# A pause after every sixteen router gathers in a graph, attention and mixture-of-experts kernel

## What is computed

```python
h = (x_flat @ W_gat).reshape(M, HEADS, NUM_EXPERTS)
a_src = (h * att_src).sum(-1)
a_dst = (h * att_dst).sum(-1)
e = jax.nn.leaky_relu(a_src[src] + a_dst[dst], negative_slope=0.2)
e_max = jax.ops.segment_max(e, dst, num_segments=M)
ee = jnp.exp(e - e_max[dst])
denom = jax.ops.segment_sum(ee, dst, num_segments=M)
alpha = ee / (denom[dst] + 1e-16)
msg = h[src] * alpha[:, :, None]
agg = jax.ops.segment_sum(msg, dst, num_segments=M).reshape(M, HEADS * NUM_EXPERTS) + b_gat
...
topk_s, topk_i = jax.lax.top_k(scores, TOP_K)
w = jax.nn.softmax(topk_s, axis=-1)
...
for ei in range(NUM_EXPERTS):
    g = jnp.where(topk_i == ei, w, 0.0).sum(-1)
    hh = jax.nn.gelu(x @ W1[ei] + b1[ei], approximate=False)
    out = out + g[..., None] * (hh @ W2[ei] + b2[ei])
```

## Time and profile before

| | |
|---|---|
| median of 3 runs | 5559.33 us |
| lowest and highest | 5557.41 and 5565.59 us |
| the profiled execution, its own time | 5560.58 us |
| its span in the profile | 5558.8 us |
| mean granted TensorE clock | 0.801 |
| busy: PE, DVE, ACT, POOL | 63%, 37%, 14%, 51% |
| gathers of line 1353 | 1024 |

### The profile page before, as it was taken

How to read it: one execution, slowest core, us unless ns; L and a number is a source line. 1 busy time by engine, 2 the same in 40 slices (tenths; PEclk the granted TensorE clock), 3 DMA queues, 4 the chain that set the end, 5 groups by cost and what they waited for, 6 DMA issues and landing times. The chain is left out here.

```text
span 5558.8 us, 46231 instructions
## 1 busy us (share of the span) xinstructions
PE 3511.5 (63%) x12937; PEld 2291.2 (41%) x12938; DVE 2083.0 (37%) x4892; ACT 802.4 (14%) x1970; POOL 2839.8 (51%) x2937
## 2 busy tenths in 40 slices
PE   0688888888577767777242766666666666669300
PEld 0455555555455545555121443434343434346200
DVE  5455566565566555444010111112011111103278
ACT  4111111111011111111010101111111111112000
POOL 2666666666666666666657144444445353530420
PEclk6898999899788888888675888788877878789755
DMA  7444444444455555655121111111111111111297
GB/s 254 116 112 111 114 113 113 110 112 111 112 133 148 148 145 149 166 152 151 20 62 19 32 46 35 42 39 43 38 42 46 35 46 36 46 31 63 87 255 257
DMA packets 381413, 540.56 MB, mean 97 GB/s; under 512 B 120315, under 2 KB 297819, under 8 KB 381144
## 3 DMA queue, kind: packets, MB, share of 16 engines
q0 software_dynamic: 119136, 234.44, 19.2%
q1 hardware_dynamic: 243119, 288.12, 16.2%
q10 hardware_dynamic: 19016, 16.48, 0.9%
HBM read 392.03 MB, written 146.74 MB: 97 GB/s over the span
## 5 line engine op out<-in xcount | busy, mean ns | idle before, releaser
L787 POOL DMA_INDIRECT rows<-xn_rows,gsrc x1664 | 1611.5, 968 | 902.0 <-issue 458.8
L1353 POOL DMA_INDIRECT nb<-route_rows,idx x1024 | 1001.5, 978 | 1087.4 <-DVE msg L1428 772.7
L1092 PE MATMUL PS<-rows,oh 128*128 128x257 f32 x3328 | 908.3, 426 | 339.9 <-issue 215.3
L1682 PE MATMUL PS<-arena,hid 128*125 128x256 f32 x3200 | 773.2, 400 | 524.3 <-ACT hid L1643 311.5
L1674 PE MATMUL PS<-x2g,arena 128*128 128x500 f32 x1600 | 759.4, 634 | 314.8 <-issue 154.5
L1682 PEld LDWEIGHTS PS<-arena,hid 128*125 128x125 f32 x3200 | 633.5, 199 | 680.5 <-issue 577.6
L1092 PEld LDWEIGHTS PS<-rows,oh 128*128 128x128 f32 x3328 | 693.4, 214 | 470.9 <-issue 284.3
L1617 DVE TENSOR_TENSOR y_sb<-PS,b_b 125x512 f32<-125x512 f32 x200 | 128.7, 686 | 2010.5 <-PE PS L1682 1466.4
L1674 PEld LDWEIGHTS PS<-x2g,arena 128*128 128x128 f32 x1600 | 321.2, 204 | 732.1 <-issue 540.1
L1643 ACT ACTIVATE hid<-PS,b_sb 128x500 f32<-128x500 f32 x400 | 270.2, 678 | 1551.1 <-PE PS L1674 762.5
L1164 PE MATMUL PS<-own_w,p_t 128*125 128x512 f32 x400 | 228.8, 656 | 77.6 <-ACT s_t L1052 45.4
(11 more groups left out here) (304 smaller groups left out, 3088.6 us busy)
## 6 DMA issues: line engine op xcount, KB each, us to landing
y_rows<-y_sb SPq DMA_DIRECT2D x100, 512.0 KB
arena<-y_rows SPq DMA_DIRECT2D x100, 512.0 KB
rows<-xn_rows,gsrc POOLq DMA_INDIRECT x1664
nb<-route_rows,idx POOLq DMA_INDIRECT x1024
sum_rows<-kept SPq DMA_DIRECT2D x104, 128.5 KB
x_rows<-x SPq DMA_DIRECT2D x100, 128.0 KB
hid<-x_rows SPq DMA_DIRECT2D x100, 128.0 KB
m_in<-sum_rows SPq DMA_DIRECT2D x100, 125.5 KB
```

The source lines that it names most:

```text
L787: pool.indirect_dma_start(out=rows[w][h][:, q, 0:D], out_offset=None, in_=xn_rows, in_offset=bass.IndirectOffsetOnAxis(ap=gsrc[:, s * HU + ...
L1092: last = mm(SUM[:, 0:D + 1], oh[w][h][:, q, :], rows[w][h][:, q, :], start=h == 0 and q == 0, stop=h == 1 and q == HU - 1)
L1353: pool.indirect_dma_start(out=nb[b % NBUF][:, c, :], out_offset=None, in_=route_rows, in_offset=bass.IndirectOffsetOnAxis(ap=idx[:, b * W ...
L1682: last = mm(Y[j % 2][e // 2][0:NP, (e % 2) * D:(e % 2 + 1) * D], hid[:, 4 * e + k, j * NP:(j + 1) * NP], w2_sb[:, e, k, :], start=k == 0, ...
```

## The change

With `REST = 16`, every sixteenth gather of line 1353 no longer waits for the gather four before it but for all four semaphores, that is until every gather issued so far has landed. The very first gather of all is left out. The other gathers wait as before. No instruction is added, removed or moved, and the tables and buffers stay as they are.

```diff
@@ -48,6 +48,7 @@
 AHEAD = 4
+REST = 16
 EVEN = 112
@@ -1348,7 +1349,10 @@
                     if b >= NBUF:
                         pool.wait_ge(s_nbf, b - NBUF + 1)
                     for c in range(W):
-                        if b or c >= AHEAD:
+                        if (b or c) and c % REST == 0:
+                            for q in range(AHEAD):
+                                pool.wait_ge(s_nb[q], (b * W + c) // AHEAD * 16)
+                        elif b or c >= AHEAD:
                             pool.wait_ge(s_nb[c % AHEAD], (b * W + c) // AHEAD * 16)
                         pool.indirect_dma_start(out=nb[b % NBUF][:, c, :], out_offset=None, in_=route_rows,
                                                 in_offset=bass.IndirectOffsetOnAxis(ap=idx[:, b * W + c:b * W + c + 1], axis=0)
```

## The result

| | before | after |
|---|---|---|
| median | 5562.46 us (4 runs) | 5330.73 us (4 runs) |
| lowest and highest | 5557.41 and 5567.54 us | 5323.38 and 5332.99 us |
| span of the profiled execution | 5558.8 us | 5331.2 us |
| mean granted TensorE clock | 0.801 | 0.821 |

The ratio is 0.9581, with a 95% interval of 0.9567 to 0.9596. The change takes 232 us off, where the prediction had 180. The lines of the changed file stand four further down: the gather is line 1357, the first layer 1678, the second 1686, the gelu 1647, `msg` 1432.

The account below looks back on a forecast made before the run. Gathers issued faster than their shared cost were taken to squeeze PE in the expert stage. Thirteen bursts giving 130 us, the first 22, and 10 to 50 from running ahead became -180: 5560 - 180 = 5380 us, range 4690 to 5480.

Parts of the forecast that it names:

- What bounds the kernel: Expert stage: PE alone needs 1388 of 2347 us; 959 are lost while GpSimd's gathers run.
- the backlog: Gathers cost 1.40 us of something shared, issued each 1.25: each adds 0.15 us, served one us per us in pauses.
- The pause: GpSimd's wait at every sixteenth gather: adds 1.2 to 1.96 us, taken as 1.45, 50 times.
- The curve of the squeeze: PE's us per matmul by backlog: none below about 1.8, 0.87 at 2.0, 1.58 at 2.6, 2.80 from 4.7.
- the squeeze: While gathers run, and somewhat after, all that PE completes comes through at 2.80 us a matmul at worst.
- The sum: Expert stage: some 10 us for each of 13 bursts, 22 for the first, plus running ahead: -180 us; chance 0.58.
- PE running ahead: Expert stage: what PE can make up by running ahead of its completions adds 10 to 50 us of gain.
- What costs nothing: Waits beginning batches 3 to 15, 13 places: hidden under VectorE's until the cover shrinks from 59 us to about 2.
- The pauses clear it all: Rival: pauses empty whatever is full, the squeeze never starts, GpSimd bounds the expert stage: 4317 instead of 5188, -870; chance 0.22.
- Slower: Rival: backlog not served in pauses, bursts' added 72 us are squeezed, PE loses 62 us: 5622; chance 0.12.
- No effect: Rival: gathers do not cause the squeeze, or clearing and longer bursts cancel: 5560; chance 0.08.
- What would show it: Signs: 50 idles of 1.5 to 1.8 us, gelus after 4 to 9, PE free within 4, stage 2165, clock above 0.80.

Follow-up runs that it names:

- experiment 11: Kernel before with only the first four of each batch's 64 columns gathered, the rest of `nb` zero: 4573.89 us against 5513.75, one run.
- experiment 1: Kernel before with three memsets of a spare tile ahead of every sixteenth gather, no new wait: 5417.69 us against 5573.19, ratio 0.9722.
- experiment 6: Kernel before with one memset of 2100 columns ahead of every sixteenth gather, instead of three of 700: 5439.28 us against 5562.36, ratio 0.9785.
- experiment 5: Changed kernel with `REST = 12`, a pause after every twelve gathers: 4946.88 us against 5562.36 for the kernel before, ratio 0.8881.
- experiment 2: Changed kernel with `REST = 8`, a pause after every eight gathers: 4876.00 us against 5573.19 for the kernel before, ratio 0.8743.
- experiment 9: Kernel before with a memset of 350 columns ahead of every gather, an even pace without pauses: 4862.39 us against 5513.75, ratio 0.8820.
- experiment 12: Changed kernel with pauses after every ten gathers and every ten graph-stage scatters: 4769.63 us against 5513.75 for the kernel before, ratio 0.8653.
- experiment 10: Changed kernel with pauses after every eight gathers and every eight graph-stage scatters: 4811.14 us against 5513.75 for the kernel before, ratio 0.8729.
- experiment 7: Kernel before with gathers of 64 rows instead of 128, the other half of `nb` zero: 5591.35 us against 5562.36, one run.
- experiment 4: Kernel before with `AHEAD = 2`, two gathers under way at most instead of four, no pauses: 5358.26 us against 5573.19, ratio 0.9610.

## Why the prediction was right, and where it was not

**What bounds the kernel.** This part held in every number that could be tried. The loss of 959 us against PE alone was measured directly: with few gathers PE's work takes 950 us less (experiment 11). The cost of a gather came out of the changed kernel again: behind the slow gather of batch 3 PE is free (3276.71 - 3189.64) / 62 = 1.404 us per gather later, against 1.405 before. The 1.405 was read from a gelu and the 1.404 from PE; from PE's own rows the kernel before gives (3305.91 - 3217.39) / 62 = 1.428, so the cost is known to some 0.03 us. And the backlog is served one us per us: three pauses moved the last gather back by 5.7 us and did not move PE's release back with it, 87.07 us after the same gather where it was 88.52. In the median of the 12 later bursts it went from 87.1 to 86.5 us. So PE is free 4.0 us behind the burst, and the prediction named 4.

**The pause.** This step failed. The prediction took that a pause adds 1.45 us, by the row of 1.5 us for a scatter that is waited for, and named 1.96 as the upper bound, by the row of 2.26 us. The pauses add 1.97. The row that was nearest in kind (a wait for a gather, in the same stage, while others are under way) was the better one. DMA: Bandwidth & Descriptors in the Trainium skill (Anatomy of one DMA), with its fixed cost of about 2.0 us, would have given 1.7 us added as an estimate; the trace has 1.97 for gathers and 1.89 - 0.30 = 1.59 for scatters.

**The curve of the squeeze.** This step failed as well, the other way. Read over one burst without pauses, it had no squeeze below a backlog of 1.8 us and 0.87 us per matmul at 2.0. In the changed burst the backlog at 3222 us is, by the same arithmetic, 16 x 0.15 - 1.97 + 10.6 x 0.15 = 2.0 at most, and the gelu interval there is 5.71 us, 1.43 per matmul where the curve has 0.87. At the end of the burst it is between 3.4 (by the arithmetic) and 4.0 (by the release), and PE goes at 2.80 in places where the curve has 2.0 to 2.4. So the squeeze doesn't depend on the backlog alone, as this arithmetic counts it; in this burst it came back earlier and harder after a pause than it had come at first. The rows do not say by what. The other bursts fit: experiments 1 and 6 have the change's pace and lose more.

**The sum.** The two errors have opposite signs. With 1.97 and the old curve the sum was -430 to -600, with 1.45 it was -180, and -232 was measured. Term by term: the loss in a single burst went from 55.5 us to 40.1 in the mean where the sum had 55 and 44, so 13 bursts gave 200 us for 130 (the sum's own 55 - 44 = 11 would have made it 143). The first burst gave 28 us by the same count (over 280 us) and 17 when it was changed alone, for 22. Together, 200 and 28, these are 228 of the 232 us, which leaves nearly nothing for PE running ahead, where the sum had added 10 to 50 us. The prediction was near by its mechanism and partly by luck in its sizes.

**What costs nothing.** The 13 waits at the beginning of batches 3 to 15 are hidden under VectorE's, which still are 8.0 to 84.2 us long. The cover shrank as the prediction said it could; with pauses each eight it is gone.

**The rivals.** "The pauses clear it all" did not happen at sixteen, and its reason against held word for word: 1.4 x 16 = 22.4 us do not fit into the time that sixteen gathers and a pause take, 16 x 1.25 + 1.97 = 21.97. With twelve it is 16.8 against 16.97, just enough at 1.40 and not at the 1.43 that PE's own rows give (17.2), and the squeeze is nearly gone (experiment 5); with ten 14.0 against 14.47 (14.3 at 1.43), and there the case came about, with GpSimd as the bound, as the rival had it. "Slower" fell: the backlog is served in pauses, and a burst that is longer by 6 us is no loss. "No effect" fell with the result, and with experiments 2, 9 and 11. SBUF — State Buffer in the Trainium skill (Who interferes with whom) says that a DMA never contends with a compute engine. Here 960 gathers, left out, are worth 940 us. The section speaks of the memory's ports, and no run here shows a port; read as a rule for a whole kernel, it is contradicted by these runs.

**What would show it.** The pauses are longer than the 1.5 to 1.8 us named. In batch 3 the gelus from 25 us on came after 3.6 to 7.1 us with close ones behind the pauses (named: 4 to 9). The stage is 2133 us by its own ends against 2360 by the same ends before, 227 less (named: 182 less). The clock is 0.82 in the stage (named: above 0.80).

## What to carry to other kernels

When an engine slows down in a stretch with rows that wait for nothing visible, look at what GpSimd issues meanwhile, and when the slowdown ends: if it outlasts the burst, there is a backlog, and its cost per instruction can be read from the last idle time to the engine's release. A burst of more than some ten instructions at a pace under that cost should be slowed down to a little above it, here by 0.05 to 0.1 us, by pauses or evenly; it pays even where the issuing engine becomes the bound, but no slower than needed then (over the whole stage 1.52 us a gather beats 1.55 and 1.58: experiments 12, 10 and 9). A pause that is nearly enough brings little (0.958 at 1.38 us a gather), one that is just more than enough nearly all (0.865 with ten, scatters included, at 1.48). Do not carry a response curve that was read from one pattern of load over to another.

## What the runs showed of the hardware

- An indirect gather of GpSimd costs 1.40 us of something that TensorE's and ScalarE's progress shares (1.405, 1.390 and 1.407 us before, 1.404 after; 1.428 before by PE's own rows), and GpSimd can issue one each 1.25. With 64 rows instead of 128 the squeeze is no smaller (experiment 7).
- At a steady 1.25 us the others slow down after some fifteen gathers, to 2.80 us a matmul, and stay slow 11 us past 64 gathers and 27 us past 192. With pauses each twelve, at 1.44 us, traces of it are left; with pauses each ten, in bursts of 1.46 to 1.55 us, apart from waits for the gathers, two intervals are left, of 2.3 and 3.4 us. Which unit is shared was not tried.
- From the end of a gather's instruction to the start of the next it takes 2.27 us when GpSimd waits for the gather just issued, and at most 1.64 to 1.77 us when it waits for the one two before (experiment 4). For a scatter it is 1.89 us (experiment 10).
- The granted clock fell with the squeeze: 0.51 in the squeezed stretch of the first burst, the lower of the two levels (1.2 GHz of 2.4) nearly throughout, and 1.00 in the same stretch with the pace slowed, where PE is busy for 166 of 170 us. The lower clock costs a little beyond the burst too: the 128 matmuls of the second layer behind batch 3 took 30.36 us, at 0.91 of the clock, against 27.89.
